# Denominators from sums of four key blocks, values by eight heads, and longer strips of exponentials

## The reference

```
x = x + 0.5 * ffn0(ln(x))       # hidden 1536, weights rounded to fp8
x = x + attn0(ln(x))            # 16 query heads, 4 key/value heads, rotary, biases
x = x + 0.5 * ffn0(ln(x))
x = x + 0.5 * ffn1(ln(x))       # hidden 2048
x = x + attn1(ln(x))            # 16 heads with their own keys and values
x = x + 0.5 * ffn1(ln(x))
```

## Time and profile before

| | |
|---|---|
| median of 3 runs | 2652.11 us (2651.18 to 2652.96) |
| the profiled execution | 2646.1 us, its span 2644.4 us |
| TensorE busy | 2543.7 us, 96% of the span |
| VectorE, ScalarE, GpSimd busy | 56%, 40%, 37% |
| the chain that ended last | 81% TensorE, 6% VectorE, 3% GpSimd, 3% ScalarE, 2% SP |
| granted TensorE clock, mean | 0.99 |

### The profile page before, as it was taken

The page is one execution under the profiler, slowest core; times in us unless marked ns, Lnnn a source line. Parts: engine busy times, 40 slices in busy tenths (PEclk is TensorE's granted clock), DMA queues, the critical chain, the costliest instruction groups (busy, mean ns, idle before and its releaser), DMA issues.

```text
span 2644.4 us, 43617 instructions
## 1 busy us (share of the span) xinstructions
PE 2543.7 (96%) x16928; PEld 2016.4 (76%) x16928; DVE 1472.0 (56%) x2780; ACT 1045.2 (40%) x1901; POOL 969.1 (37%) x1357
## 2 busy tenths in 40 slices
PE   6999989899999999999999999999999899999999
PEld 4788867667668888888888878776777678888887
DVE  7777578878875445433333345787578643333333
ACT  7555346655653223311111133566456532211111
POOL 3333566666653335211111122666366521111110
PEclk9999989999999999999999999999999999999999
DMA  4222131122130110100000002333132100000001
GB/s 148 72 72 72 38 76 45 47 65 65 45 100 0 37 44 9 41 25 24 24 24 25 24 16 57 90 93 77 45 94 68 47 33 24 24 24 25 24 16 64
DMA packets 71997, 128.69 MB, mean 49 GB/s; under 512 B 15728, under 2 KB 24944, under 8 KB 71792
## 3 DMA queue, kind: packets, MB, share of 16 engines
q1 hardware_dynamic: 71792, 125.92, 16.6%
HBM read 62.42 MB, written 13.63 MB: 29 GB/s over the span
## 4 chain that ended last, share of the span: by engine, by line
PE 81%; DVE 6%; POOL 3%; ACT 3%; issue 2%; SPq 2%; DMA 1%; DVEq 0%; ACTq 0%; POOLq 0%
PE psum L1018 66%; PE psum L1103 4%; PE psum L1140 4%; PE psum L1121 4%; PE psum L1151 2%; DVE psum L1472 2%; SPq L1697 1%; PE psum L1027 1%; SPq L1716 1%; POOL rstd L1575 1%; POOL s4a1e L1623 1%; POOL s1a0e L1623 1%; ACT s1a0e L1306 1%; DVE stats L1338 0%; ACT s4a1e L1306 0%
## 5 line engine op out<-in xcount | busy, mean ns | idle before, releaser
L1472 DVE CUSTOM_DVE_ANT_0 psum<-psum,mask_q 128x512 f32<-128x512 f32 (+7 forms) x512 | 385.5, 766 | 170.4 <-PE psum L1103 168.4
L1018 PE MATMUL psum<-hA_hi,wmem 128*128 128x256 f32 (+1 forms) x1536 | 405.2, 334 | 0.9 <-ACT s4a1e L1306 0.8
L1018 PEld LDWEIGHTS psum<-hA_hi,wmem 128*128 128x128 f32 x1536 | 270.2, 190 | 31.9 <-ACT s4a1e L1306 1.4
L1018 PE MATMUL psum<-hA_lo,wmem 128*128 128x512 f32 (+1 forms) x864 | 293.5, 340 | 0.0
L1306 ACT ACTIVATE s4a1e<-psum,p_scale 128x384 f32<-128x384 f32 (+5 forms) x384 | 204.9, 580 | 82.7 <-PE psum L1121 80.3
L1306 ACT ACTIVATE s1a0e<-psum,p_scale 128x384 f32<-128x384 f32 (+5 forms) x384 | 201.6, 579 | 73.2 <-PE psum L1121 72.6
L1425 DVE SCALAR_TENSOR_TENSOR x<-psum,x 128x512 f32<-128x512 f32 x256 | 175.8, 689 | 97.3 <-PE psum L1018 93.8
L1396 DVE TENSOR_TENSOR s5f1prod<-psum,s5f1silu 128x512 f32<-128x512 f32 x64 | 44.3, 692 | 302.0 <-PE psum L1018 302.0
L1396 DVE TENSOR_TENSOR s3f1prod<-psum,s3f1silu 128x512 f32<-128x512 f32 x64 | 44.3, 692 | 294.1 <-PE psum L1018 294.1
L1587 POOL TENSOR_TENSOR wmem<-raw,wmem 128x512 fp32r<-128x512 f32 x58 | 74.3, 1291 | 326.1 <-ACT wmem L1208 326.1
L1018 PE MATMUL psum<-s3f1w,s3f1a 128*128 128x512 f32 x768 | 181.6, 390 | 0.9 <-POOL s3f1w L1587 0.9
(11 more groups left out here) (192 smaller groups left out, 5515.2 us busy)
## 6 DMA issues: line engine op xcount, KB each, us to landing
s1a0qst<-s1a0qs SPq DMA_DIRECT2D x96, 128.0 KB, 2.4
s4a1qst<-s4a1qs SPq DMA_DIRECT2D x96, 128.0 KB, 2.5
s4a1kst<-s4a1ks SPq DMA_DIRECT2D x96, 128.0 KB, 2.4
raw<-in_gate SPq DMA_DIRECT2D x44, 256.0 KB, 2.8
raw<-in_up SPq DMA_DIRECT2D x44, 256.0 KB, 2.8
raw<-in_down SPq DMA_DIRECT2D x44, 256.0 KB, 2.8
rounded<-s0f0w SPq DMA_DIRECT2D x24, 256.0 KB, 2.0
s2f0w<-rounded SPq DMA_DIRECT2D x24, 256.0 KB, 5.0
```

The source lines that it names most:

```text
L1018: ins = pe.matmul(out_, w, m, start=n == 0, stop=n == len(terms) - 1)
L1472: dve.tensor_tensor_reduce(scores, scores, mask_q[:, SEQ - width:SEQ].rearrange("p (z w) -> p z w", z=scores.shape[1]), -1.0, -MASKED, ALU ...
```

## The change

1. **Sums of four.** After every fourth block a new step `e_sum` (GpSimd) adds the strip of the third block (which holds the sum of the third and fourth) to that of the first: 768 and 256 columns wide. `v` gets a second subtraction: in each four tiles, the third less the first (`v_dif`; the earlier one is now `v_odd`). `den` is made for each four blocks instead of each two: groups of 256 and 128 columns stay, those of 192 and 64 go. Every `pv` of a four waits for that four's `e_sum`; a strip is free when the fourth block's product is done.
2. **Values of `a1` for eight heads at a time.** `v_tile` has 256 columns; there are four sets of eight tiles (two per sequence). The first stands ahead of the first key, the others in groups 1, 3 and 5, every second unit from 14. Their weights are two pieces per set, in the second slot of `wmem`: the first set's loaded in the stage before, the others' at units 4 and 6 of the same group. q and k weights of `a1` keep the first slot alone; those of group 1 are now loaded and split just ahead of the first values.
3. **Longer strips.** `e32` has 11264 columns in `a0` and 11776 in `a1`; the tiles `vw` of `a1` are gone.
4. **Other units.** `QK_W_AT` 20 to 17, `O_W_AT` 23 to 30; the stage after an attention stage also waits for the last `e_sum`.

```diff
-QK_W_AT = 20
-O_W_AT = 23
+QK_W_AT = 17
+O_W_AT = 30
-PV_LAG = 9
+PV_LAG = {"a0": 9, "a1": 9}
+PV_BY = {"a0": 2, "a1": 2}
+V_AT = 14
+V_STEP = 2
+V_W_AT = 4
-E32 = 7680
+E32 = {"a0": 11264, "a1": 11776}
+HALVES, VH = 2, 8
...
-        return group_weights(s, 0) + group_weights(s, 1)
+        return group_weights(s, 0) + (group_weights(s, 1) if STAGES[s] == "a0" else
+                                      v_weights_of(s, 0))
...
         side = Beside(plan)
+        if not grouped:
+            for job in group_weights(s, 1):
+                side.start(job)
         side.waiting += values(0)
...
-            put(values(1), HEADS * ST + (PV_LAG + 1) // 2 * 2 - 8, 1)
+            for vp in range(1, BATCH * HALVES):
+                put(v_weights_of(s, vp), (2 * vp - 1) * UNITS + V_W_AT, 2)
+                put(values(vp), (2 * vp - 1) * UNITS + V_AT, V_STEP)
...
             plan.append(("pv", s, n, jt))
-            if jt % 2 == 0:
-                plan.append(("den", s, n, k))
-                return
-            if k == PAIRS - 1:
+            if jt % HPG == 0:
+                plan.append(("den", s, n, jt // HPG))
+            if jt == ST - 1:
...
             if i % 2:
                 plan.append(("e_add", s, n, i // 2))
+            if i % HPG == HPG - 1:
+                plan.append(("e_sum", s, n, i // HPG))
...
-            return sem["pv"], at("pv", "pv", s, n, jt | 1)
+            return sem["pv"], at("pv", "pv", s, n, jt | (HPG - 1))
...
-                on.wait_ge(sem["e_add"], at("e_add", "e_add", s, n, jt // 2))
+                on.wait_ge(sem["e_sum"], at("e_sum", "e_sum", s, n, jt // HPG))
...
-                e = quarters(s, n, 2 * k)
+                e = quarters(s, n, HPG * k)
                 for c in range(HPG):
-                    ins = pe.matmul(psum[c * HD:(c + 1) * HD, bank, QUAD + 2 * k * HD:CH],
+                    ins = pe.matmul(psum[c * HD:(c + 1) * HD, bank, QUAD + HPG * k * HD:CH],
                                     ones[:], e[:, :, c, :], start=False,
-                                    stop=k == PAIRS - 1, skip_group_check=True)
+                                    stop=k == QUADS - 1, skip_group_check=True)
...
-                                  ALU.subtract).then_inc(sem["v_dif"], 1)
+                                  ALU.subtract).then_inc(sem["v_odd"], 1)
+                if tiles.stop % HPG:
+                    return
+                on.wait_ge(sem["v_odd"], at("v_odd", "v_out", s, b, t))
+                dve.tensor_tensor(v[:, tiles.stop - 2, :, :], v[:, tiles.stop - 2, :, :],
+                                  v[:, tiles.stop - HPG, :, :],
+                                  ALU.subtract).then_inc(sem["v_dif"], 1)
...
+            def e_sum(s, n, k):
+                begin, end = e32_place[s, n, HPG * k]
+                more, more_end = e32_place[s, n, HPG * k + 2]
+                e32 = T[s]["e32"]
+                on.wait_ge(sem["e_add"], at("e_add", "e_add", s, n, 2 * k + 1))
+                pool.tensor_tensor(e32[:, begin + 2 * P:end], e32[:, begin + 2 * P:end],
+                                   e32[:, more:more_end], ALU.add).then_inc(sem["e_sum"], 1)
```

More of the change, by code:

```diff
@@ L147, in group_weights, with v_weights_of @@
         return [split(s, n, g, 0) for n in names_of_group(s, g)]
+    def v_weights_of(s, vp):
+        return [split(s, "v", vp, i) for i in range(2)]
     def first_weights(s):
@@ L238, in attention @@
         v_weights = Beside(plan)
-        v_weights.waiting += [split(s, "v", 0, k) for k in range(1 if grouped else KT)]
+        v_weights.waiting += [split(s, "v", 0, 0)] if grouped else []
         def group_jobs(g):
@@ L344, in attention @@
                 plan.append(("e_add", s, n, i // 2))
+            if i % HPG == HPG - 1:
+                plan.append(("e_sum", s, n, i // HPG))
             behind.append((n, i))
-            if len(behind) > PV_LAG and i % 2 == 1:
-                times_v(*behind.pop(0))
-                times_v(*behind.pop(0))
+            if len(behind) > pv_lag and i % pv_by == pv_by - 1:
+                for _ in range(pv_by):
+                    times_v(*behind.pop(0))
             for job in beside.pop(u, []):
@@ L409, in raised @@
     if kind == "v_out":
[L410 to L411 removed]
+        return ("v_out", "v_odd", "v_dif") if STAGES[step[1]] == "a0" else \
+            (("v_out",), ("v_odd",), ("v_out",), ("v_odd", "v_dif"))[step[3] % HPG]
     if kind == "piece_out":
@@ L521, in run @@
         elif kind == "v_tile":
-            done[step] = work("pe", 2.8, *banks)
+            done[step] = work("pe", 1.4, *banks)
         elif kind == "v_chunk":
@@ L546, in run @@
         elif kind == "e_add":
-            done["sum", s, *where] = work("pool", (SEQ - (2 * where[1] + 1) * P) / 400)
+            done[step] = work("pool", (SEQ - (2 * where[1] + 1) * P) / 400)
+        elif kind == "e_sum":
+            done["sum", s, *where] = work("pool", (SEQ - (HPG * where[1] + 2) * P) / 400)
         elif kind == "e_mask":
@@ L951, in read_by @@
             if kind == "v_turn" or kind == "v_tile" and step[3] % 2:
-                return sem["v_dif"], at("v_dif", "v_out", *step[1:])
+                return sem["v_odd"], at("v_odd", "v_out", *step[1:])
             if kind == "v_tile":
@@ L980, in head_of, with v_of, v_before @@
             return (HPG * j + g, j, j) if STAGES[s] == "a0" else (n % HEADS, j, n % HEADS)
[L982 to L983 removed]
+        def v_of(s, n, jt):
+            return (n // HEADS, jt // CT) if STAGES[s] == "a0" else \
+                (n // VH, jt | (HPG - 1))
         def v_parts(s, b, t):
[L987 to L991 removed]
+            first, n = (0, KV0) if STAGES[s] == "a0" else (b % HALVES * VH, VH)
+            tiles = slice(t * CT, (t + 1) * CT) if n == KV0 else slice(t, t + 1)
+            fill = (("v_turn", s, b, t), "v_tp") if n == KV0 else (("v_tile", s, b, t), "v_mm")
+            cols = (tiles.stop - tiles.start) * n * HD
+            src = psum[:, banks[fill[0]][0], 0:cols].rearrange("p (t h d) -> p t h d", h=n, d=HD)
+            return fill, tiles, src, T[s]["v"][:, :, first:first + n, :]
+        def v_before(s, b, tile):
+            ahead, heads = (1, HEADS) if STAGES[s] == "a0" else (HALVES, VH)
+            return (sem["pv"], at("pv", "pv", s, (b - ahead + 1) * heads - 1, tile)) \
+                if b >= ahead else None
         def halves(ps, width):
```

96 lines of the change are left out of this document (49 added, 47 removed).

## The result

The changed kernel takes 2696.6 us (median of 4 runs, 2693.2 to 2707.5) where the kernel before, on the same chip, took 2652.5 (4 runs, 2651.2 to 2655.4): ratio 1.0172, 95% interval 1.0148 to 1.0196, so **some 46 us slower**. The forecast was 4 us faster, and the time lies beyond the range (2668). The profiled execution took 2699.4 us, its span 2697.7.

A forecast was written before the change was run, and what follows sets the result against it. TensorE, busy 96% of the span, was taken as the bound. -28.8 + 7 + 7.6 + 3 + 17.8 - 10 = -3.4 us, so 2648 us against a median of 2652.1; range 2627 to 2668.

The forecast's parts named there:

- Denominators: Both attention stages: removing the 192 and 64 column matmuls saves TensorE 0.45 us for each of 64 heads, -28.8 us.
- Sums: GpSimd, both stages: two more adds a head, 2.6 us; priced through tails +7, normalisations +7.6 and bias adds +3.
- Normalisations: First stage: ScalarE waits 21.6 us more for GpSimd's normalisation work behind sums; a third reaches TensorE, +7.6 us.
- Tails: Ends of both stages, GpSimd back to back: sums and handshakes, plus the moved output weight split, +7 us, bounds 3 and 10.
- Bias adds: First stage, groups 0 and 4: eight bias adds each build up GpSimd backlog, +3 us, bounds 0 and 15.
- some 4.5 us of backlog are borne before TensorE waits: First values product of a head: its lag of about 9.5 us leaves this much slack for GpSimd running late.
- C: GpSimd bounds the first stage and normalisation groups; TensorE waits over 15 us a stage for sums; 2667, full price 2675; chance 0.22.
- The price for VectorE beside a busier GpSimd: VectorE's two-SBUF-input subtractions blocked by GpSimd: 1 us, hidden; at worst 45 us, near 2660, chance 0.04.
- The hold ahead of the second stage: Ahead of the second stage's first key: ScalarE idles about 17 us on late q weights, first key +5.5 us.
- B: Rival: no ScalarE hold ahead of the first key, and GpSimd's backlog stays inside the slack; 2629 us, chance 0.28.
- Values later and loads moved: Second stage's values made later, +12.3 us; weight loads at other units spare ScalarE's waits in both stages, -10 us.
- D: Rival: removed denominator matmuls free nothing, since column tiles overlap; +25 us, 2677, chance 0.05.

The follow-up runs named there:

- e2: The kernel before without the denominator matmuls of pairs 2 and 4 (192 and 64 columns): 2639.4 us, ratio 0.9955.
- e1: The changed kernel with each e_sum adding only two columns, all waits and order kept: 2660.2 us, ratio 1.0046.
- e7: The changed kernel with sums of four undone (pairs, all denominators); values by eight heads, long strips and moved loads stay: 2661.8 us, ratio 1.0048.
- e10: The kernel before with the 192 and 64 column denominator matmuls made twice: 2673.5 us, ratio 1.0087.
- e12: The changed kernel with pairs, group 1's q and k loads ahead of the stack transfers, and loads at units 20 and 23: 2646.3 us, ratio 0.9989.
- e4: The kernel before with the q and k loads at unit 17 and the output weight's at 30: 2655.4 us, ratio 1.0024.
- e16: The changed kernel with sums on VectorE, three units behind GpSimd's add, group 1's loads ahead of the stacks, units 20 and 23: 2687.6 us, ratio 1.014.
- e3: The changed kernel with group 1's q and k loads issued ahead of the 24 stack transfers: 2680.7 us, ratio 1.0109.

## Why the prediction was wrong

The parts, as us of 2650:

| part | forecast | measured | by |
|---|---|---|---|
| matmuls removed | -28.8 | -11.9 | e2 |
| longer wait, no sum in it | 0 | +11.4 | e1 less (e2 + e7) |
| the sums on GpSimd | +17.6 | +33.4 | change less e1 |
| values by eight, loads moved, strips | +7.8 | +12.7 | e7 |
| sum | -3.4 | +45.6 | |

The measured column adds up by its making, since each row is a difference of runs; it does not prove that the parts are independent. Of the 49 us between forecast and result, 16.9 are the removed matmuls, 15.8 the sums, 11.4 the longer wait and 4.9 the rest.

- **Denominators: the first step that failed.** "I take it whole; the end at which its idle gaps swallow their share is -27." The size of the steps was right (28.0 us in e2's trace); taking it whole was wrong. The kernel gained only 11.9 us, since TensorE idled 13 us more and its busy time fell by 18.1 us instead of 28. A share of 6% idle does not bound what the next engine takes: e10 against e2 shows that the slope differs by the direction.
- **Sums: the second.** With the first they make two thirds of the error. Their durations were right. The groups of e_sum after:

```profile
L1673 POOL TENSOR_TENSOR s1a0e<-s1a0e 128x768 f32<-128x768 f32 x32 | 58.5, 1829 | 2.5
...
L1673 POOL TENSOR_TENSOR s1a0e<-s1a0e 128x256 f32<-128x256 f32 x32 | 23.5, 735 | 2.5
```

  I had 1.83 and 0.75 us, and "GpSimd near 370 us in the first stage": it is 378. *Normalisations* were of the right size: in the same stretch as the earlier trace rows the kernel after has

```profile
ACT tmp L1225 <- POOL shift L1620: 29.9, 13, 3.9
...
PE psum L1060 <- ACT tmp L1225: 11.4, 4, 3.5
...
PE psum L1176 <- POOL s1a0e L1673: 7.2, 4, 3.8
```

  so TensorE waits 5.7 us more there (and 2.4 more in the second stage), for 7.6 forecast. *Tails*: the last two reciprocals of the first stage are 9.4 us apart where they were 4.4, those of the second 10.9 where they were 5.1: +10.8 for +7, just beyond the bound of 10. With the two-column sums of e1 they are 6.5 apart in both stages, so a third of this growth belongs to the longer wait of the next point. The first stage's last rows on GpSimd have the output weight's split where the prediction put it:

```profile
800.95 1.27 POOL L1629 TENSOR_TENSOR s1a0ow<-raw,s1a0ow 128x512 fp32r<-128x512 f32 x1
...
803.08 0.72 POOL L1673 TENSOR_TENSOR s1a0e<-s1a0e 128x256 f32<-128x256 f32 x1
```

  *Bias adds* were priced too low in group 0, with +3 for both groups: it has two waits of 3.84 and 2.72 us and some 12 us at half clock. The step behind it is "some 4.5 us of backlog are borne before TensorE waits"; there the eight bias adds, masks and sums follow one another before the backlog is gone. In group 4, where the working had more than 100% of GpSimd, nothing of the kind happened: its bias adds run from 584 to 604 us, GpSimd is busy 51.4 of 57 us (577 to 634), no product waits for a sum, and the clock is 1.00.

  The working of the sums had no price at all for **the clock**, and this is the step of it that failed; C names the clock only as a sign. By the windows above it is about 29 us over both stages, beside 24 us of direct waits: for the sums 12.1 and 6.4 in the two stages (1.2 and 1.3 for the adds before), and for the normalisations' transposes 11.4 and 4.9 (5.7 and 2.5 before). The direct waits alone are not far above the 17.6 forecast. The added waits of e1 are among them, so waits and clock together are more than the 33.4 of the table.

  The price for VectorE beside a busier GpSimd, 45 us at the worst in C, did not come: the subtraction L1491 (L1455 before) takes 582 ns on average where it took 517, about 2 us over its 32 times.
- **A longer wait with nothing in it** stood at zero, since TensorE waited little for pairs. The table's 11.4 rests on three runs whose parts are taken to add, so it is good to some 7 us; the profiled executions of the same kernels would give 3. The mechanism that fits is that a values product of a head's first block now needs the exponentials, masks and adds of four blocks. What the traces show of it are 6.8 us more of direct waits in e1 than before, some of them in the tails. What of it is TensorE's idle time and what is slow clock (0.986 in e1, 0.988 in e7) I have not separated.
- **The hold ahead of the second stage** came out as forecast: ScalarE idle 17.5 us on raw<-in_q ("about 17"), and the way from the first stack to the first exponential 35 us for 31, so +4 for +5.5. Undoing it brought 12.6 us there, about the distance between the forecast's +17.8 and B's +5.8.
- **Values later and loads moved** were two errors that partly cancelled: the second stage of e12, with neither hold nor moved units, is only 3.9 us longer than before where I had 12.3; and the moved loads cost about 6 instead of giving 10. The waits for k's landings in the earlier trace rows (14.2 us, now 6.0 over the run) went down as I said, without bringing time. ScalarE's waits for the output weight's landings rose instead, from 3.1 to 20.1 us over the run (22.4 in e4), which the working had put at nothing; so ScalarE waited as much as before, elsewhere.
- **The rivals.** C comes nearest, "GpSimd becomes the bound"; it had 0.22. Its own sign did not show, though: TensorE waited for the sums 12.1 us in one stage and 6.4 in the other, not "more than 15 us in a stage". Its terms put the sums at 7 + 21.6 + 15 = 43.6 us, more than the 33.4 measured (36.6 less 10.6 is 26.0, not the 22.6 of its text; its 2675 has the 26). And still it lies 22 us too low: the matmuls, the longer wait and the rest are 33 us too cheap in it, the sums 10 too dear. With the measured -11.9 it would have said 2692, which is near by luck, since the other two errors then cancel. That GpSimd at its limit cancels a gain on TensorE is my reading; no run takes the matmuls away or puts them back beside the full load of GpSimd. B needed the backlog to stay inside the slack, and it did not. D, that the matmuls free nothing since column tiles overlap, is refuted by the steps of e2 (674 to 349 ns), though 59% of what I counted did not come back.

A cheaper form of the sum on GpSimd was not tried, so whether sums of four can pay with less than 2.5 us a head stays open.

## What to carry to other kernels

Work moved from an engine at 96% to one at 70% is not free because 30% is left: look at its worst stretches, with its bursts (here the bias adds of the first group, the normalisations, and the end of each stage), and price the backlog there. The same bursts in another group, with as many bias adds, cost nothing, so look at each. Here the new waits of TensorE were paid about twice, as 21.9 us idle and as 19.2 us of slower work (the change against e1). And test a removed cost alone, both ways (remove it, double it), before counting it whole: here it gave 41% of its estimate, although its steps had been read rightly.

## What the runs showed of the hardware

- After TensorE had been busy 2.2 us in 6 (365 to 371 us), its granted clock was 0.50 (1.2 GHz) for the 12 us that followed, in which TensorE was itself busy 9.3 us; full speed came back in the slice of 383 to 386.
- On VectorE, an add of 256 columns with both inputs in SBUF took 1167 ns on average, and up to 2248, where it started while a `tensor_tensor` of GpSimd was running (40 adds of e16), and 419 to 426 ns otherwise (24 adds).
- Asking an in-order engine for a result a little early cost much more than the work: the kernel with the 128 sums on VectorE stood at +227 us with them right behind GpSimd's add and at +37 with them three units later, both with e3's edit (the second with units 20 and 23 too).
- Taking 28.0 us of matmuls away from a TensorE that was busy 96% of the time gave 11.9 us (e2); adding the same matmuls cost 23.1 (e10).
